# A gated attention and mixture-of-experts kernel on Trainium2: the head of the program reordered

## The reference

```python
x = x + jnp.tanh(g_xattn[0]) * _L0_xattn_ref(_layernorm(x), ctx_1024, ctx_1024, w_q, w_k, w_v, w_o)
x = x + jnp.tanh(g_ffn[0]) * _L0_ffn_ref(_layernorm(x), router_w, rms_w, w1, w2, rms_w_s, w1_s, w2_s)
```

## Time and profile before

| what | value |
|---|---|
| median of 3 runs | 136.04 us (134.81, 136.04, 136.25) |
| the profiled execution, its time | 134.85 us |
| the profiled execution, first to last instruction (span) | 133.0 us |
| mean granted clock of TensorE in it | 0.987 |
| busy: PE, DVE, ACT, POOL | 122.8, 77.9, 64.3, 44.8 us |

### The profile page before, as it was taken

One profiled execution on the slowest core, in us unless ns is written; L12 is line 12 of the kernel. 1 busy time (PEld: TensorE's weight loads), 2 busy tenths in 40 slices (PEclk: granted clock), 3 DMA queues, 4 the chain that ended last, 5 costly groups with the idle time before them and its releaser, 6 DMA issues.

```text
span 133.0 us, 2399 instructions
## 1 busy us (share of the span) xinstructions
PE 122.8 (92%) x809; PEld 102.8 (77%) x809; DVE 77.9 (59%) x200; ACT 64.3 (48%) x108; POOL 44.8 (34%) x76
## 2 busy tenths in 40 slices
PE   7897959979999999999999998995799999999992
PEld 7796837839449737945976998994699999999991
DVE  0048896678858848976892143599644433333473
ACT  4063336666959667595566416942022343222220
POOL 4008998000000100000010037876255567667000
PEclk9999999999999999999997699999999999999999
DMA  4999999999500000000000000000000000000002
GB/s 117 353 319 415 421 412 417 443 415 428 222 0 2 5 0 0 0 0 0 5 0 0 5 0 0 7 2 0 0 0 0 0 0 0 0 0 0 0 5 69
DMA packets 3104, 13.50 MB, mean 102 GB/s; under 512 B 430, under 2 KB 1006, under 8 KB 2710
## 3 DMA queue, kind: packets, MB, share of 16 engines
q1 hardware_dynamic: 3094, 13.37, 26.0%
HBM read 13.14 MB, written 0.23 MB: 101 GB/s over the span
## 4 chain that ended last, share of the span: by engine, by line
PE 75%; DVE 14%; DMA 5%; issue 2%; SPq 1%; ACT 1%; DVEq 0%
PE score_ps L692 17%; PE attn_ps L570 12%; PE score_ps L509 5%; PE ring L537 5%; PE ring L552 5%; PE ring L554 5%; DMA x_space<-in_x_rows_dram 5%; PE ring L685 4%; PE ring L686 4%; PE ring L687 4%; DVE xn_rows L972 3%; PE ring L484 3%; PE ring L486 2%; PE ring L485 2%; PE score_ps L504 2%
## 5 line engine op out<-in xcount | busy, mean ns | idle before, releaser
L692 PE MATMUL score_ps<-w,mixT 128*112 (+1 forms) x232 | 28.1, 273 | 2.6 <-DVE xn_rows L1177 2.3
L692 PEld LDWEIGHTS score_ps<-w,mixT 128*112 128x112 f32 x232 | 27.2, 177 | 3.6 <-issue 3.0
L903 ACT ACTIVATE mixT<-ring 128x896 f32<-128x896 f32 x16 | 14.6, 918 | 29.5 <-PE ring L687 29.5
L1177 DVE SCALAR_TENSOR_TENSOR xn_rows<-score_ps,gates,xn_rows 112x128 f32<-112x128 f32 x52 | 14.7, 344 | 19.7 <-PE score_ps L692 19.5
L423 POOL TENSOR_TENSOR h_scale<-h_base,minus_half 112x1 f32<-112x1 f32 x4 | 2.2, 550 | 53.8 <-DVE h_base L1035 53.8
L570 PE MATMUL attn_ps<-wkq_space,mixT 128*112 128x128 f32 x128 | 16.3, 290 | 0.0
L570 PEld LDWEIGHTS attn_ps<-wkq_space,mixT 128*112 128x112 f32 x128 | 15.7, 191 | 0.6 <-issue 0.6
L386 POOL TENSOR_TENSOR w_full<-w,columns 128x256 f32 (+1 forms) x16 | 9.8, 614 | 14.0 <-PE ring L687 12.9
L685 PE MATMUL ring<-hT_hi,w_hi 128*128 128x448 f32 (+2 forms) x36 | 13.9, 387 | 0.1
L687 PE MATMUL ring<-hT_hi,w_lo 128*128 128x448 f32 (+2 forms) x36 | 12.6, 349 | 0.0
L686 PE MATMUL ring<-hT_lo,w_hi 128*128 128x448 f32 (+2 forms) x36 | 12.6, 349 | 0.0
(11 more groups left out here) (137 smaller groups left out, 206.0 us busy)
## 6 DMA issues: line engine op xcount, KB each, us to landing
ctx_all<-in_ctx_dram SPq DMA_DIRECT2D x4, 1500.0 KB, 16.0
w<-in_w_dram SPq DMA_DIRECT2D x2, 1792.0 KB, 26.1
wkq_space<-in_wkq_dram SPq DMA_DIRECT2D x2, 512.0 KB, 4.7
wvo<-in_wvo_dram SPq DMA_DIRECT2D x1, 1024.0 KB, 8.0
w<-in_w_shared_dram SPq DMA_DIRECT2D x2, 256.0 KB, 15.1
ctx_headT<-in_ctx_headT_dram SPq DMA_DIRECT2D x1, 224.0 KB, 5.7
x_space<-in_x_rows_dram SPq DMA_DIRECT2D x1, 224.0 KB, 6.2
ctx_head<-in_ctx_head_dram SPq DMA_DIRECT2D x1, 224.0 KB
```

The lines of the kernel that those rows point to most:

```text
L692: last = nc.tensor.matmul(dst, hidden[slot][:, c, t * ROWS:(t + 1) * ROWS], w2_chunk(c), start=(c == 0), stop=(c == 1))
L903: nc.scalar.activation(hidden[slot], ring[:, 2 * slot:2 * slot + 2, 0:TOKENS], ACT.Silu).then_inc(S["hidden_ready"], 1)
L1177: last = nc.vector.scalar_tensor_tensor(out=moe[:, t, :], in0=score_ps[0:ROWS, slot, t * D:(t + 1) * D], scalar=gate(t), in1=before[:, t, ...
```

## The change

- `WARM_PRODUCTS` goes from 31 to 38.
- PE: K0 to K7 come ahead of the transposes of xn (before: K0 to K5), `scores(0, 0)` stands behind K10 (before: K9), and `scores(0, 1)` stands between M1 and M2 (before: ahead of M0).
- DVE: A0, `ctx_headT_lo` and A1 come ahead of the moments of the layer norm, A2, A3 and K1 behind them. At the first softmax, M1 is evacuated ahead of `softmax_shift(0, [1])`, and M3 ahead of its normalisation.
- ACT: A0 is evacuated ahead of `ctx_headT_hi`. Both sums of squares of batches 0 and 1 stand behind the second exponential. The copy into the second half of `ctx_stack` is gone.
- POOL: `mask_full`, `causal_all`, `xnT` and `probs_stack` are filled at the start, and all masks and constants are done ahead of the wait for the variance. The power follows. `ctx_stack` and `ctx_lo` wait for `xn_ready`. The zeros into `ctx_stack` are gone.
- The host lays `ctx_head` out as 120 x 8 x 128 (rows, eight rows of zeros, rows again) instead of 56 x 8 x 128, and POOL copies it into `ctx_stack` in one instruction.

```diff
-    + [f"K{s}" for s in range(6)] + ["xnT"] + [f"K{s}" for s in range(6, HEADS)]
+    + [f"K{s}" for s in range(8)] + ["xnT"] + [f"K{s}" for s in range(8, HEADS)]
...
-WARM_PRODUCTS = 31
+WARM_PRODUCTS = 38
...
-        ctx_head = sb("ctx_head", [Q, B, D])
+        ctx_head = sb("ctx_head", [STACK, B, D])
...
-            nc.gpsimd.memset(xnT[:, :, :], 0.0).then_inc(S["slots_zero"], 1)
             nc.gpsimd.memset(mask_full[:, :], 0.0)
             nc.gpsimd.memset(causal_all[:, :, :], 0.0).then_inc(S["causal_zero"], 1)
+            nc.gpsimd.memset(xnT[:, :, :], 0.0).then_inc(S["slots_zero"], 1)
+            nc.gpsimd.memset(probs_stack[:, :, :].bitcast(FP32), 0.0)\
+                .then_inc(S["probs_stack_zero"], 1)
...
             nc.gpsimd.memset(half[:, :], 0.5).then_inc(S["moe_consts_ready"], 1)
+
+            pool.wait_ge(S["moe_consts_ready"], 1)
+            pool.wait_ge(S["ln1_var_ready"], 1)
+            nc.gpsimd.tensor_tensor(ln_rstd[:, :], ln_var[:, :], minus_half[:, :], ALU.pow)\
+                .then_inc(S["ln1_rstd_ready"], 1)
...
-            nc.gpsimd.memset(ctx_stack[:, :, :].bitcast(FP32), 0.0).then_inc(S["ctx_stack_zero"], 1)
-            nc.gpsimd.memset(probs_stack[:, :, :].bitcast(FP32), 0.0)\
-                .then_inc(S["probs_stack_zero"], 1)
-            pool.wait_ge(S["ctx_stack_zero"], 1)
+
+            pool.wait_ge(S["xn_ready"], 1)
             pool.wait_ge(S["ctx_head_loaded"], 16)
-            nc.gpsimd.tensor_copy(ctx_stack[0:Q, :, :], ctx_head[:, :, :])\
+            nc.gpsimd.tensor_copy(ctx_stack[:, :, :], ctx_head[:, :, :])\
...
+                if g == 2:
+                    for s in (14, 15):
+                        pe.wait_ge(*evacuated(f"K{s}"))
+                    scores(0, 1)
                 wait_bank_free(pe, f"M{g}")
...
+            evacuate_own(["A0"])
             act.wait_ge(S["ctx_headT_loaded"], 16)
...
-            evacuate_own(["K10"])
-
-            act.wait_ge(S["ctx_stack_zero"], 1)
-            act.wait_ge(S["ctx_head_loaded"], 16)
-            nc.scalar.activation(ctx_stack[SLOT:STACK, :, :], ctx_head[:, :, :], ACT.Copy)\
-                .then_inc(S["ctx_repeat_ready"], 1)
-            evacuate_own(["K12"])
+            evacuate_own(["K10", "K12"])
             softmax_exp(0, 0)
-            evacuate_own(["K14"])
-            context_squares([0])
-
-            softmax_exp(0, 1)
-            evacuate_own(["M0", "M2"])
+            evacuate_own(["K14", "M0"])
...
-            context_squares([1])
+            evacuate_own(["M2"])
+            softmax_exp(0, 1)
+            context_squares([0, 1])
...
+            evacuate_own(["A0"])
+            dve.wait_ge(S["ctx_headT_hi_ready"], 1)
+            nc.vector.tensor_tensor(ctx_headT_lo[:, :], ctx_headT[:, :],
+                                    ctx_headT_hi[:, :].bitcast(FP32), ALU.subtract)\
+                .then_inc(S["ctx_headT_lo_ready"], 1)
+            evacuate_own(["A1"])
             dve.wait_ge(S["x_loaded"], 16)
             moments(x_rows)
...
-            evacuate_own([f"A{g}" for g in range(GROUPS)] + ["K1"])
+            evacuate_own(["A2", "A3", "K1"])
...
+            evacuate_own(["M1"])
             softmax_shift(0, [1])
-            evacuate_own(["M1"])
+            evacuate_own(["M3"])
             softmax_normalise(0, [1])
-            evacuate_own(["M3"])
...
-        "ctx_head": head.transpose(1, 0, 2),
+        "ctx_head": np.concatenate([rows, np.zeros((SLOT - Q, B, D), rows.dtype), rows]),
```

More of the change, by code:

```diff
@@ L258, in build @@
             squares_done guard_max_ready guard_rows_ready guard_ready
-            ctx_stack_zero probs_stack_zero ctx_hi_ready ctx_lo_ready ctx_repeat_ready
+            probs_stack_zero ctx_hi_ready ctx_lo_ready
             warm_ready table_loaded h_base_ready h_scale_ready g_h_scale_ready g_h_ready g_moment_steps
@@ L377, in _ @@
             nc.gpsimd.tensor_copy(mask[:, :], mask_full[:, :])
+            pool.wait_ge(S["ident_ready"], 1)
             nc.gpsimd.tensor_copy(ident_r[:, :], ident[:, :]).then_inc(S["causal_ready"], 1)
@@ L400, in scale_w1_static @@
                 scale_w1(e % 2, e, w1[:, e, :], rms_cols[:, e:e + 1])
-            nc.gpsimd.memset(ctx_stack[:, :, :].bitcast(FP32), 0.0).then_inc(S["ctx_stack_zero"], 1)
-            nc.gpsimd.memset(probs_stack[:, :, :].bitcast(FP32), 0.0)\
-                .then_inc(S["probs_stack_zero"], 1)
-            pool.wait_ge(S["ctx_stack_zero"], 1)
+            pool.wait_ge(S["xn_ready"], 1)
             pool.wait_ge(S["ctx_head_loaded"], 16)
-            nc.gpsimd.tensor_copy(ctx_stack[0:Q, :, :], ctx_head[:, :, :])\
+            nc.gpsimd.tensor_copy(ctx_stack[:, :, :], ctx_head[:, :, :])\
                 .then_inc(S["ctx_hi_ready"], 1)
             pool.wait_ge(S["ctx_hi_ready"], 1)
-            nc.gpsimd.tensor_tensor(ctx_lo[:, :, :], ctx_head[:, :, :],
+            nc.gpsimd.tensor_tensor(ctx_lo[:, :, :], ctx_head[0:Q, :, :],
                                     ctx_stack[0:Q, :, :].bitcast(FP32), ALU.subtract)\
@@ L487, in project_keys @@
                     .then_inc(S["ring_filled"], 1)
-            for s in range(6):
+            for s in range(8):
                 project_keys(s)
@@ L513, in scores @@
                 last.then_inc(S["scores_ready"], 1)
-            for s in range(6, 10):
+            for s in range(8, 11):
                 project_keys(s)
@@ L522, in _ @@
             scores(0, 0)
-            for s in range(10, HEADS):
+            for s in range(11, HEADS):
                 project_keys(s)
-            for s in (14, 15):
-                pe.wait_ge(*evacuated(f"K{s}"))
-            scores(0, 1)
             def transpose_probs(t):
@@ L793, in _ @@
                 .then_inc(S["ctx_headT_hi_ready"], 1)
-            evacuate_own(RING_JOBS[:RING_JOBS.index("K2")])
+            evacuate_own(["A1", "A2", "A3", "K0"])
             for g in range(GROUPS):
@@ L964, in _ @@
                 .then_inc(S["ln1_var_ready"], 1)
-            dve.wait_ge(S["ctx_headT_hi_ready"], 1)
-            nc.vector.tensor_tensor(ctx_headT_lo[:, :], ctx_headT[:, :],
-                                    ctx_headT_hi[:, :].bitcast(FP32), ALU.subtract)\
-                .then_inc(S["ctx_headT_lo_ready"], 1)
-            evacuate_own([f"A{g}" for g in range(GROUPS)] + ["K1"])
+            evacuate_own(["A2", "A3", "K1"])
             dve.wait_ge(S["ln1_rstd_ready"], 1)
@@ L1047, in subtract_hi @@
                                         ALU.subtract).then_inc(ready, 1)
-            evacuate_own(RING_JOBS[RING_JOBS.index("K2"):RING_JOBS.index("K10")])
+            evacuate_own(["K3", "K5", "K7", "xnT", "K9"])
             softmax_shift(0, [0])
@@ L1274, in layouts @@
     head = i["ctx_1024"][:, :Q, :]
+    rows = head.transpose(1, 0, 2)
     wk, wq = (by_head(i[f"L0_xattn_w_{w}"]).reshape(P, 2, CHUNKS // 2, D) for w in "kq")
```

5 lines of the change are left out of this document (removed).

## The result

| | before | after |
|---|---|---|
| median | 135.43 us (4 runs, 134.71 to 136.25) | 131.24 us (128.63, 128.94, 133.54, 133.72) |
| the profiled execution, its time and span | 134.85, 133.0 us | 128.63, 126.8 us |
| mean granted clock in it | 0.987 | 1.000 |

The ratio is 0.951, with an interval of 0.939 to 0.963: faster. The forecast was 132.6 us with 130.6 to 134.2. The median lies in that range, between two runs 1.7 to 2.0 us under it and two inside it near its top.

A forecast was written before the change was run, and what follows sets the result against it. PE bounds the kernel, working through nearly all of 133.0 us. Gains 1.1 + 1.6 + 0.95 + 1.05 less 1.4 and 0.6 make 2.7: 134.85 to 132.15, placed at 132.6 for run spread; range 130.6 to 134.2.

The forecast's parts named there:

- the named waits: PE's idle times before: 0.61 us for `wkq`, 0.89 ahead of K0, 1.46 ahead of xn's transposes, 0.81 ahead of `scores(0, 1)`.
- Start of K0: First K product: A0 and `ctx_headT_lo` evacuated earlier, so it starts at 10.0 instead of 11.08 without waiting; gain 1.1 us.
- xn: Layer norm's four normalisations on DVE: 0.34 us each with POOL waiting, ready at 14.7 instead of 19.16; gain 1.6 us.
- The clock: K products on PE: the rise from 1.2 to 2.4 GHz comes at 13.85 us; gain 1.05 us.
- rival 1: Clock rises during the A products, A2's evacuation then holds K2 1.4 us; 1.5 us more gained, 131.1 us; chance 0.27.
- The move of M0 and M1: Ahead of `scores(0, 1)`: covers K15's evacuation, gaining 0.95 us, but PE waits 1.4 us more behind the scores.
- The squares: ACT's two sums of squares, about 1.5 us each, delay P0.0's evacuation ahead of the first mix; cost 0.6 us.
- What is gained there I take to reach the end: Behind the first `mix_context` product: old order, engine hardly waits, so the 2.7 us gained by then carries through.
- one dip more or less: Clock dip during one `attention_out`, 5.03 us instead of 3.75, can fall on either kernel; forecast placed between.
- A dip of the clock that the old order has not: Listed among the signs that would show the prediction wrong; no size or place given.
- The host's layout: `ctx_head` load grows by 256 KB ahead of `wvo`, which still lands before M at 23.4; costs nothing.

The follow-up runs named there:

- old_warm38: The kernel before with 38 warm-up products instead of 31 and nothing else; ratio 0.995 (0.990 to 1.000), the same.
- old_pool_new: The kernel before with POOL's new order alone, the zeros into `ctx_stack` kept and filled at the start; ratio 0.965.
- new_pool_old: The changed kernel with POOL's work in its old order, power first and copy not waiting for xn; ratio 0.947, by the medians 0.961.
- new_warm31: The changed kernel with 31 warm-up products instead of 38; ratio 0.951 from its two short runs, by the medians 0.985.
- squares_late: The changed kernel with `scores(0, 1)` ahead of M0 and old orders around it, but both squares still behind the second exponential; ratio 0.991.
- old_layout: The kernel before with the host's 120-row layout alone, ACT's copy into `ctx_stack` gone; 132.25 to 135.61 us, by the medians 0.991.

## Why the prediction was right, and where it failed

The direction and the named waits were right. The size was off: the profiled execution gained 6.2 us, not 2.7. Of the 3.5 us between, 1.8 had come by the first mix and 1.7 came behind it.

*Start of K0.* "So K0 could start at 10.0": that rests on "A's 32 instructions cover 5.10 us", the slow pace. It started at 8.55, when `ctx_headT_lo` was done, after 0.61 us of idle time that the text had ruled out. DVE's order frees it, as said: old_warm38 without that order waits 3.05 us there.

*xn.* Forecast 4 x 0.34, with POOL as the cause. Measured 335 to 342 ns, and old_pool_new shows the cause by itself. What the text did not see is that POOL's move isn't needed once DVE's order has brought the normalisations ahead of POOL's long writes (new_pool_old).

*The clock: the step that failed.* "I take 13.85, in between and nearer to the row." It rose at 4.68, so rival 1 is what happened, and somewhat earlier than it said: in the warm-up, not during A. Its head came out within 0.6 us (K0 8.7 against 8.55, K2's wait for A2 1.4 against 0.93, transposes 15.2 against 14.68, mix 31.6 against 31.31). The mistake in weighing it was to take one execution's rise for the kernel's. In the five profiles with 31 products the rise is at 3.88, 9.31, 9.75, 9.93 and 17.14; in the eleven with 38 it is at 4.0 to 6.7. In the sum the term was 1.05; all 16 slow K products at the fast pace are 16 x 0.18 = 2.9, or 1.85 more, and K0 came 1.45 earlier than forecast. Of these 3.3 us 1.1 went to K2, which starts 1.29 us behind the product before it instead of 0.20, and 0.4 to M0 and M1 (1.64 instead of 1.4) and to the stretch behind T (7.04 instead of 6.85). That leaves the 1.8 us at the mix.

*The move of M0 and M1* was put at + 0.95 - 1.4, with the 1.4 paid as a wait. Measured 0.81 saved and 1.22 of waiting behind. *The squares* were put at 0.6 and measured 0.95. Both signs were right. The text counted them as small losses; without both the mix is at 30.34 in spite of K0's later start.

*"What is gained there I take to reach the end"* failed too, in both directions. The stretch behind the mix took 97.23 us before and 95.49 after, on the same code in the same order, because the profile of before had one stretch at 1.2 GHz (71.8 to 75.2 us) and that of after none. Profiles without such a stretch took 95.5, with one of 3.4 us 97.1 to 97.2, with two 98.8. That is 1.74 of the 6.2 us. It was in the text as "one dip more or less", 1.3 us by the earlier trace rows, put between the two cases, as 0.45 us added to the forecast.

*The price of a wait* was taken as its length. "A dip of the clock that the old order has not" stands under what would prove the text wrong, but no term or rival had it: the change, with a wait of 0.95 us that the text priced at 0.6, took 133.5 us or more in five of ten runs, about 5 us above its shortest. new_warm31's profile shows the low stretch, and squares_late beside its filled version shows that the wait brings it. For the change's own runs of 133.54 and 133.72 us there is no trace. Their mean clock of 0.961 is that of the two profiles with the long low stretch, but three short ones of 3.4 us have nearly the same (old_warm38's profile: 0.962), so for them this is inferred and not shown. The median of 131.24 lies between two groups, and that it is near rival 1's 131.1 is chance.

*The host's layout* was put at nothing; old_layout agrees within what these runs can tell.

Open: the short stretches at 1.2 GHz at 66 to 80 and at 88 to 98 us, in code that no edit touches, come in some executions and not in others. What decides that was not tried. Nor is it settled why 31 warm-up products raised the clock at 3.9 us in one profile and at 17.1 in another, nor what made single runs of 137 us.

## What to carry to other kernels

Price a new wait of TensorE not by its length alone: ask what the clock does behind it, above all ahead of products like the mix's, which start 0.40 us apart at the full clock, and fill it with cheap products if it can't be closed. When an engine gets faster in one stretch, work out who is late next at the fast pace, since here a further reordering of DVE only moved the wait, from 0.93 us in one place to 1.10 in two. And read the level of the clock from more than one execution before putting a term on it.

## What the hardware showed that was not expected

- A wait of 1.55 us, followed by mix products, brought 10.24 us at 1.2 GHz in the profiled run, and all six runs took 133.6 to 135.1 us. Waits of 3.05 and 2.65 us in old_warm38, followed by K products, each brought 3.4 us. A wait of 1.55 us ahead of K0 in old_layout brought none: the clock stayed up until 19.55, a microsecond behind the end of another wait, of 3.31 us. So the length of a wait alone does not tell what it costs; that it is the products behind it that decide is not shown, as no run changed them alone. The Trainium skill, "TensorE: Matmul & The Clock Gate", section "A second HAM failure mode: psum-queue depth-cycling", tells of short idle times between groups of matmuls that make the clock swing; the trace agrees, with waits of 0.95 and 1.22 us in new_warm31 and 1.55 in squares_late.
- 24 products of zeros (1.51 us) in the wait of squares_late held the clock at 1.00 in the profiled run.
- Mix products of 448 columns start 0.40 us apart at the granted clock of 1.00 and 0.67 apart at 0.50, while K products of 448 columns start 0.20 and 0.38 apart.
- POOL's fill, cast and subtraction cost a DVE instruction up to 2.2 us beside a length of 0.34, while POOL's own lengths hardly moved (the cast of 56 rows 1.03 us alone and 1.09 beside DVE, the subtraction 2.40 and 2.36).
